# Holding GpSimd's large instructions until each layernorm has been applied, in a small vision tower

## What is computed

```
x = patch_embedding(im) + conv_b                          # 256 tokens x 128
for l in 0, 1:
    q, k, v = split((LN(x) * g1 + b1) @ qkv_w[l])           # 8 heads x 64
    q = softmax(q, head axis) / 8;  k = softmax(k, token axis)
    x = x + (q @ (k^T v)) @ out_w[l] + out_b[l]
    x = x + gelu((LN(x) * g2 + b2) @ ff1_w[l] + ff1_b[l]) @ ff2_w[l] + ff2_b[l]
h = (LN(x) * gf + bf) @ head_w + head_b                   # 256 tokens x 192
h = h + linear_attention(LN(h)) @ W_out + b_out
h = h + gelu_tanh(LN(h) @ W0^T + b0) @ W1^T + b1          # W0, W1: mixed masks times weights
```

## Time and profile before

| | |
|---|---|
| time, median of 3 runs | 151.41 us (151.07 to 154.46) |
| span of the profiled execution | 154.1 us |
| its own time | the run of 154.46 us, the only one longer than its span |
| PE busy, PEld busy | 131.1 us (85%), 113.1 us (73%) |
| DVE busy | 93.7 us (61%) |
| ACT busy | 66.0 us (43%) |
| POOL busy | 49.1 us (32%) |
| HBM traffic | 74 GB/s over the span |

### The profile page before, as it was taken

One profiled execution on the slowest core, in us unless ns is written; L12 is line 12 of the kernel. 1 busy time (PEld: TensorE's weight loads), 2 busy tenths in 40 slices (PEclk: granted clock), 3 DMA queues, 4 the chain that ended last, 5 costly groups with the idle time before them and its releaser, 6 DMA issues.

```text
span 154.1 us, 2173 instructions
## 1 busy us (share of the span) xinstructions
PE 131.1 (85%) x790; PEld 113.1 (73%) x790; DVE 93.7 (61%) x236; ACT 66.0 (43%) x149; POOL 49.1 (32%) x60
## 2 busy tenths in 40 slices
PE   1699889999779989799797996769987959999993
PEld 1468668797658968589576984559876948999992
DVE  1200087947799668977689757773957796145201
ACT  3010313906559746697375981144222040163230
POOL 0000020074162953447553673180671060004000
PEclk9999999999999999999999999956977995599999
DMA  5999997008800000000000000000000000000101
GB/s 161 285 421 415 421 412 262 0 4 265 209 0 0 6 0 0 0 0 4 0 0 0 0 4 0 0 0 2 2 0 0 4 0 0 0 4 0 51 0 51
DMA packets 3388, 11.50 MB, mean 75 GB/s; under 512 B 393, under 2 KB 1385, under 8 KB 3122
## 3 DMA queue, kind: packets, MB, share of 16 engines
q1 hardware_dynamic: 3378, 11.37, 20.6%
HBM read 10.98 MB, written 0.39 MB: 74 GB/s over the span
## 4 chain that ended last, share of the span: by engine, by line
PE 55%; DVE 26%; issue 5%; POOL 5%; ACT 3%; DMA 3%; SPq 0%; DVEq 0%; ACTq 0%; POOLq 0%
PE bank L302 16%; DVE xn L655 10%; PE bank L320 10%; PE bank L437 5%; PE bank L389 5%; PE bank L561 5%; POOL rstd L1103 3%; DMA embed_sb<-in_embed 3%; DVE stats L645 2%; DVE yT_hi L662 2%; DVE nkmax L695 2%; POOL yT_lo L1109 1%; PE bank L336 1%; PE bank L531 1%; PE bank L339 1%
## 5 line engine op out<-in xcount | busy, mean ns | idle before, releaser
L1103 POOL TENSOR_TENSOR rstd<-var,minus_half 128x2 f32<-128x2 f32 x14 | 10.2, 726 | 69.8 <-DVE var L650 69.8
L655 DVE TENSOR_SCALAR xn<-x,mv,rstd 128x128 f32<-128x128 f32 x20 | 13.8, 732 | 4.2 <-POOL rstd L1103 4.2
L320 PE MATMUL bank<-embed_sb 128*128 128x256 f32 x32 | 12.0, 544 | 4.4 <-DMA embed_sb<-in_embed 4.4
L955 ACT ACTIVATE yT<-bank,small_sb 128x256 f32<-128x256 f32 x10 | 5.7, 565 | 19.5 <-DVE yT_hi L662 16.4
L320 PEld LDWEIGHTS bank<-embed_sb 128*128 128x128 f32 x32 | 8.5, 277 | 7.2 <-DMA embed_sb<-in_embed 5.1
L1122 POOL TENSOR_TENSOR qn<-q,rqsum 128x512 f32<-128x512 f32 x8 | 8.2, 1044 | 15.2 <-DVE rqsum L719 15.2
L336 PE MATMUL bank<-small_sb,xn 128*128 128x128 f32 x20 | 4.4, 301 | 7.6 <-DVE xn L655 7.6
L413 PE MATMUL bank<-cw,qT 128*128 128x128 f32 x64 | 10.0, 289 | 0.4
L413 PEld LDWEIGHTS bank<-cw,qT 128*128 128x128 f32 x64 | 8.2, 190 | 2.0 <-issue 1.3
L336 PEld LDWEIGHTS bank<-small_sb,xn 128*128 128x128 f32 x20 | 2.0, 141 | 10.3 <-DVE xn L655 10.3
L975 ACT ACTIVATE kexp<-bank,nkmax 128x256 f32<-128x256 f32 x16 | 7.4, 473 | 4.3 <-DVE nkmax L695 4.3
(11 more groups left out here) (142 smaller groups left out, 349.1 us busy)
## 6 DMA issues: line engine op xcount, KB each, us to landing
embed_sb<-in_embed SPq DMA_DIRECT2D x3, 768.0 KB, 7.9
patches_sb<-in_patches SPq DMA_DIRECT2D x2, 1024.0 KB, 12.1
restw<-in_rest_w SPq DMA_DIRECT2D x2, 768.0 KB, 16.1
qkvw<-in_qkv_w SPq DMA_DIRECT2D x3, 256.0 KB, 11.0
embed_sb<-in_qkv_w SPq DMA_DIRECT2D x1, 768.0 KB, 4.7
embed_sb<-in_embed SPq DMA_DIRECT2D x1, 576.0 KB, 4.4
projw_raw<-in_proj_w SPq DMA_DIRECT2D x1, 576.0 KB, 16.2
embed_sb<-in_fc_w SPq DMA_DIRECT2D x1, 576.0 KB, 7.6
```

Source lines behind the costliest of these rows:

```text
L320: mm = nc.tensor.matmul(dst[:, 0:TOKENS], embed_sb[:, c, 0:D], rhs, start=(c == 0), stop=(c == KCONV - 1))
L655: last = nc.vector.tensor_scalar(xn[i][:, t, 0:width], src[:, t, 0:width], mv[i][:, t, 0:1], rstd[i][:, t:t + 1], ALU.subtract, ALU.mult)
L1103: nc.gpsimd.tensor_tensor(rstd[i][:], var[i][:], minus_half[:], ALU.pow).then_inc(rstd_ready[i], 1)
```

## The change

A new helper on GpSimd, `after_norm(i, n)`, waits for xn_ready, the semaphore of `norm_apply`, and computes nothing. It is put behind every rsqrt but the very first (the one of LN1, image 0, ahead of the loop). The large instructions that stood ahead of an LN1 rsqrt or between rsqrts move behind it: qkvw_lo's second and third parts in step 1, both halves of mix_fc in step 2, aqkvw_lo's second in step 3, ff1w_lo of layer 0 in step 0, and fcw_lo's first part to after the LN2 rsqrt of the tail. In the tail, add_bias3 of image 1 (b_out) moves ahead of the LN4 rsqrt of image 0.

On VectorE, `k_max` is split in its two halves and the LN2 `norm_apply` goes between them; the LN2 statistics move from the start of step s to the end of the step before, between `add_attention` and VectorE's `norm_out_lo`.

```diff
-            def k_max(l, i):
-                for b in range(2):
-                    dve.wait_ge(k_done[i], 2 * l + b + 1)
...
+            def k_max(l, i, b):
+                dve.wait_ge(k_done[i], 2 * l + b + 1)
...
             for s in range(STEPS):
                 l, i = divmod(s, IMAGES)
                 lp, ip = divmod(s - 1, IMAGES)
-                if s:
-                    norm_stats(ip, LN2(lp), x[ip], D, x_mid[ip], lp + 1)
-                k_max(l, i)
+                k_max(l, i, 0)
                 if s:
                     norm_apply(ip, LN2(lp), x[ip], D)
+                k_max(l, i, 1)
                 q_max(l, i, 0)
...
                     add_attention(l, i)
+                    norm_stats(i, LN2(l), x[i], D, x_mid[i], l + 1)
                     norm_out_lo(1 - i, LN1(ln))
...
+            def after_norm(i, n):
+
+                pool.wait_ge(xn_ready[i], n + 1)
+
...
                 if s:
                     rsqrt(ip, LN2(lp))
+                    after_norm(ip, LN2(lp))
                     add_bias(ip, "ff2_b", lp, x_mid[ip], lp + 1)
...
+                rsqrt(1 - i, LN1((s + 1) // 2))
+                after_norm(1 - i, LN1((s + 1) // 2))
+                if s == 0:
+                    weight_low_part("ff1_0", 1, ff1w_all(0), ff1w_parts[0][0][:], ff1w_parts[0][1][:])
                 if s == 1:
                     qkv1_low_part(1)
+                    qkv1_low_part(2)
+                if s == 2:
+                    mix_fc(0)
+                    mix_fc(1)
                 if s == 3:
                     weight_low_part("aqkv", 1, aqkvw[:, 1, :], aqkvw_parts[0][:, 1, :], aqkvw_parts[1][:, 1, :])
-                if s == 2:
-                    mix_fc(0)
-                rsqrt(1 - i, LN1((s + 1) // 2))
-                if s == 1:
-                    qkv1_low_part(2)
-                if s == 2:
-                    mix_fc(1)
-                if s == 3:
-                    weight_low_part("fc", 1, fcw[:, 0, :], fcw_parts[0][:, 0, :], fcw_parts[1][:, 0, :])
-                if s == 0:
-                    weight_low_part("ff1_0", 1, ff1w_all(0), ff1w_parts[0][0][:], ff1w_parts[0][1][:])
             rsqrt(1, LN2(1))
+            after_norm(1, LN2(1))
+            weight_low_part("fc", 1, fcw[:, 0, :], fcw_parts[0][:, 0, :], fcw_parts[1][:, 0, :])
             rsqrt(0, LN3)
+            after_norm(0, LN3)
             add_bias(1, "ff2_b", 1, x_mid[1], LAYERS)
...
             rsqrt(1, LNF)
+            after_norm(1, LNF)
...
             rsqrt(1, LN3)
+            after_norm(1, LN3)
+            add_bias3(1, "b_out", rows_sb[:, ROW["b_out"]:ROW["b_out"] + E], h_ready[1])
             rsqrt(0, LN4)
+            after_norm(0, LN4)
             add_bias3(0, "b_proj", projb[:], h2_ready[0])
-            add_bias3(1, "b_out", rows_sb[:, ROW["b_out"]:ROW["b_out"] + E], h_ready[1])
             rsqrt(1, LN4)
+            after_norm(1, LN4)
```

More of the change, by code:

```diff
@@ L690, in x_from_embedding @@
                                       bankof[:, 0:TILES * D]).then_inc(x_ready[i], 1)
-            def k_max(l, i):
-                for b in range(2):
-                    dve.wait_ge(k_done[i], 2 * l + b + 1)
-                    nc.vector.tensor_reduce(nkmax[i][:, 2 * b:2 * b + 2],
-                                            KB[b][:].rearrange("p (c t) -> p c t", c=2), AX_X, ALU.max,
-                                            negate=True).then_inc(nkmax_ready[i], 1)
+            def k_max(l, i, b):
+                dve.wait_ge(k_done[i], 2 * l + b + 1)
+                nc.vector.tensor_reduce(nkmax[i][:, 2 * b:2 * b + 2],
+                                        KB[b][:].rearrange("p (c t) -> p c t", c=2), AX_X, ALU.max,
+                                        negate=True).then_inc(nkmax_ready[i], 1)
             def q_max(l, i, t):
```

## The result

The changed kernel takes 142.50 us (median of 4 runs, 140.76 to 142.78), the kernel before 152.94 us beside it: a ratio of 0.940 with a 95% interval of 0.927 to 0.953. A later series gave 0.929 (0.919 to 0.939). Medians are of all runs; ratios compare only the faster runs of each kernel, because some executions are slowed by some per cent whatever the kernel. The forecast was 143.0, range 139.5 to 147.0. The gain is 10.4 us by the medians where the sum had 8.4.

What follows compares the result with a forecast made beforehand. VectorE's normalisation xn (L655), held up by GpSimd's running instructions while TensorE waits, was taken as the bound. Terms 3.67 + 3.0 - 1.3 + 3.0 = 8.4 us off the median 151.41 gave 143.0 us, range 139.5 to 147.0.

Steps and rivals of the forecast that it cites:

- the sum: Gains and costs over LN1/LNF turns, LN2 turns, moved statistics and tail: 3.67 + 3.0 - 1.3 + 3.0 = 8.4 us.
- The base: Median 151.41 us of the kernel before, from which 8.4 was taken; the profiled run's extra 3 us put down to a clock stretch.
- the first rival: Late in the program, TensorE waits less and one more lower-clock stretch vanishes: 139.6 us; chance 0.2, both sides.
- the second rival: GpSimd's held work becomes the wait in the steps; LN2's gain of 3.0 goes, the 1.3 stays: 146.0 us; chance 0.15.
- L655 is long because of what GpSimd runs beside it: VectorE's normalisation xn waits for GpSimd's running instruction; held back, each pair falls to 0.60 us.
- The four LN1/LNF turns: xn shortens at these turns; TensorE's idle weight loads, 0.71, 0.74, 0.94 and 1.28, are gained: 3.67 us, low end 2.6.
- The LN2 turns and the moved statistics: Three steps: earlier xn between k_max's halves gains 1.0 each, 3.0; yT_lo late behind the statistics costs 0.28, 0.35, 0.65.
- A second small term: Step 1: TensorE's next product waits for the query third of qkvw_lo by at most 0.1 us.
- The credit given to VectorE's new order: LN2 turns: earlier statistics and xn between k_max's halves, rebuilt with the GpSimd holds, together gain 1.0 us a step.
- The tail: Waits at LN3 image 0 (1.38), LNF image 1 (0.22) and LN4 image 0 (1.41) all go: 3.0 us; LNF's 1.28 counted elsewhere.
- GpSimd's held work becomes the wait: In the steps, LN2's rsqrt and yT_lo queue behind late large parts; 146.0 us, chance 0.15.
- xn is long of itself: At L655 the change does not shorten xn and nothing is won: 152.7 us, slower than before; chance 0.04.

Runs made afterwards that it cites:

- experiment 1: Changed kernel's GpSimd queue (the holds) with VectorE's order of the kernel before: 141.34 us against 154.72, ratio 0.906.
- experiment 2: Changed kernel's VectorE order with the whole GpSimd queue of the kernel before: 154.80 us against 154.72, ratio 1.006.
- experiment 10: VectorE's order of the kernel before, GpSimd's queue with the holds and one large part back in steps 1 to 3: 140.85 us against 154.56, ratio 0.934.
- experiment 3: Changed kernel with VectorE's yT_lo ahead of the moved statistics again: one run, 142.88 us.
- experiment 8: Kernel before with 19 extra unread matmuls ahead of five TensorE waits in the tail: 152.13 us against 154.00.
- experiment 9: Changed kernel with yT_lo ahead of the statistics, one part back per step 1 to 3, five extra matmuls in the tail: 140.12 us against 154.56.

## Why the prediction was right, point by point

The number came out within 0.5 us, and part of that is luck: two errors cancel. The base of 151.41 was 1.5 us below the median beside the result, and the gain of 8.4 was 2.0 short of the 10.4 measured, mainly for the clock, which the sum left out. What happened is the first rival, lower-level stretches lost, to which the prediction gave a chance of 0.2 and 139.6 us. The mechanism of the sum was right term by term, with the exceptions below. One step of the range does not add up either: the second rival's 146.0 and half a microsecond make 146.5, not 147.0.

**L655 is long because of what GpSimd runs beside it.** Shown: experiments 1 and 2 separate hold and order, and at the seven LN1, LN2 and LNF turns of the loop that had been long, from step 0's LN1 on, a pair of xn takes 0.60 with the first and 1.39 to 2.07 with the second.

**The four LN1/LNF turns, 3.67.** From xn's start to yT_hi's the three LN1 turns took 2.07, 2.07 and 2.27 before (the first from the earlier trace rows) and 1.33, 1.29 and 1.30 after: 0.74, 0.78 and 0.97 where 0.71, 0.74 and 0.94 stood. This fits the choice of TensorE's loads, and not its array, as what sets the start. LNF's 1.28 lies in the tail.

**The LN2 turns and the moved statistics, 3.0 - 1.3.** From yT_hi to the next xn it took 16.01, 16.01 and 16.15 before and 15.26, 15.36 and 15.75 after. That is 0.75, 0.65 and 0.40, where 1.0 - 0.28, 1.0 - 0.35 and 1.0 - 0.65 make 0.72, 0.65 and 0.35. The size was right and a cause was off: in step 2 it was not yT_lo that was held up but var, the small instruction before it.

```profile
68.15 0.60 DVE L655 TENSOR_SCALAR xn<-x,mv,rstd 128x128 f32<-128x128 f32 x2 [0.82 <-POOL rstd L1102]
...
68.83 2.91 POOL L1146 TENSOR_TENSOR embed_sb<-embed_sb,fc_mix 96x768 f32<-96x768 f32 x2 [0.72 <-DVE xn L655]
...
70.36 0.49 DVE L645 BATCH_NORM_STATS2 stats<-x 128x6 f32<-128x128 f32 x2
...
70.76 0.30 DVE L648 BATCH_NORM_AGGREGATE mv<-stats 128x2 f32<-128x6 f32 x2
...
71.09 0.68 DVE L650 TENSOR_SCALAR var<-mv 128x2 f32<-128x2 f32 x1
...
71.69 0.41 DVE L669 TENSOR_TENSOR yT_lo<-yT,yT_hi 128x256 fp32r<-128x256 f32 x1
71.85 0.80 POOL L1102 TENSOR_TENSOR rstd<-var,minus_half 128x2 f32<-128x2 f32 x1
...
72.16 0.38 PE L302 MATMUL bank<-yT_lo,qkvw_hi 128*128 128x256 f32 x1 [0.62 <-DVE yT_lo L669]
```

GpSimd runs from 68.83 to 71.74; var, 0.17 us otherwise, takes 0.68 and ends with it. The statistics just ahead of it, bn_stats and bn_aggr, also work in SBUF and run beside the same GpSimd instructions, and they take their usual 0.49 and 0.30: not every VectorE instruction on SBUF is held up, only xn, var and yT_lo were seen to be. yT_lo behind var is free again. The product starts 2.71 after yT_hi, where 2.57 was forecast. That yT_lo itself is held up when it comes first, experiments 1 and 3 show. The Trainium skill, "SBUF — State Buffer", section "Who interferes with whom", says that VectorE's second SBUF input comes through the read interface that it shares with GpSimd. The traces of experiments 1 and 3 agree, with 0.95 and 1.34 us against 0.43.

A second small term was short: in step 1 TensorE waited 0.30 us for the query third of qkvw_lo, where at most 0.1 stood.

```profile
52.18 2.51 POOL L1160 TENSOR_TENSOR qkvw_lo<-embed_sb,qkvw_hi 128x512 fp32r<-128x512 f32 x2 [0.72 <-DVE xn L655]
...
53.50 0.50 PE L302 MATMUL bank<-qkvw_hi,yT_hi 128*128 128x512 f32 x1 [0.30 <-POOL qkvw_lo L1160]
```

**The credit given to VectorE's new order was wrong.** The prediction rebuilt the LN2 turns with both edits and called the result a gain of both. Experiments 1, 2 and 10 show that the order has no share in it worth naming. What it wins (xn earlier) it gives back (k_max's second half later, and the statistics ahead of yT_lo).

**The tail, 1.28 + 3.0 = 4.3, measured 8.1.** TensorE's waits for xn that the sum names are gone, but its wait for qn of the linear attention (L523) grew from 0.4 to 1.2 us. The rest is the clock, the first rival's direction. The windows of the tail, before and after:

```profile
core 0: us, PE busy (x) PEld busy (x) DVE busy (x) ACT busy (x) POOL busy (x), PEclk, DMA share, GB/s
92.30:151.90 59.60, 52.13 (x309) 46.84 (x307) 34.24 (x90) 17.23 (x38) 15.93 (x21) 0.86 0.01 4
```

```profile
core 0: us, PE busy (x) PEld busy (x) DVE busy (x) ACT busy (x) POOL busy (x), PEclk, DMA share, GB/s
85.20:136.70 51.50, 47.19 (x309) 42.94 (x308) 28.50 (x90) 17.31 (x38) 17.49 (x22) 0.93 0.02 5
```

Of the 8.1 us, TensorE's idle time gives 3.2 (59.60 - 52.13 = 7.5 before, 51.50 - 47.19 = 4.3 after) and its busy time 4.9, with the same 309 matmuls. The mean clock rose from 0.86 to 0.93. At half level for a share of 2 x 0.14 of 59.6 us, that is 16.7 us before, and 2 x 0.07 of 51.5, 7.2 us, after (estimates; half of the difference, 4.8, is the busy time that came back). Experiment 8 shows that 3.8 us come back in the tail with every xn there still long, when only TensorE is kept busy; experiment 9 shows it for the last stretch. So the lower level follows TensorE's idle time in the tail. How much of it the kernel before has differs from run to run: in 29 timed runs of the later series its mean clock is 0.943 to 0.988, median 0.955, while the changed kernel's ten have 0.975 to 0.988. The profile before, at 0.945, is near the low end, so that 4.9 us is more than this term gives in most runs. Which wait brings on which stretch stays open.

**The base.** The forecast went from the median of 151.41. The kernel before spread from 149.6 to 157.0 in the later series, with medians of 154 to 154.7; the 3 us between its runs were put down to one stretch in the tail. The embedding, up to 2.8 us between profiled runs of the same code, is at least as good a cause, and the prediction did not see it.

**The rivals.** That GpSimd's held work becomes the wait came true in small: the first yT_lo product was 0.5 us later in step 2 and 0.1 later in step 1 than in step 0, and there was the 0.3 above. That xn is long of itself is refuted by experiment 1.

## What to carry to other kernels

When one line's instructions of one shape differ several times in length, lay the other engine's timeline beside them before anything else; a large GpSimd instruction that is not urgent belongs behind the VectorE instruction on the path, but only as much of it as ends before the next VectorE instruction that it holds up, small ones too (here xn, var and yT_lo, but not the statistics). Put the rest into the stretch where GpSimd is idle (here 2.5 us in each step): in the loop that was worth 0.6 us alone and 1.5 together with yT_lo ahead of the statistics. Where the clock line falls behind a wait that is taken from TensorE, the gain can be more than the wait: here 4.3 us of waits went with 8.1 in one pair of profiles. Put it into the range, since the kernel before lost more or less to it from run to run.

## What the runs showed of the hardware

A VectorE addition of 128x2 elements (var) was held up to the end of GpSimd's instruction, 0.68 us instead of 0.17, while bn_stats and bn_aggr beside the same instruction were not (0.49 and 0.30 for two, as elsewhere). A VectorE subtraction with both inputs in SBUF was held up by a running GpSimd instruction, 1.34 instead of 0.43, and GpSimd's power beside such a subtraction took 0.80 instead of its usual 0.70. k_max, which reads PSUM, took 0.68 to 0.69 beside GpSimd's xb sum and weight parts as without them. TensorE's first 32 matmuls ran at a median of 634 ns in one profiled run and 379 in another, the same code. TensorE's lower clock level in the tail became rarer when extra matmuls filled its waits: a mean clock of 0.966 to 0.989 in four runs against 0.944 to 0.966.
